# Causal mask inside VectorE's maximum pass, the first products of a batch in another order, and attend's hi and lo values made by GpSimd

## The reference

```python
x = _rmsnorm(hidden_states, ln1_w)
attn = _attention(x, Wq, Wk, Wv, Wo)
mod = MOD_SCALE * jnp.tanh(attn @ A)
h = _rmsnorm(residual, ln2_w)
gate_pre = h @ W_in_base.T + mod * (h @ A) @ B
gate = jax.nn.silu(gate_pre)
up = h @ W_up_base.T
mlp_out = gate * up @ W_down.T
return residual + mlp_out
```

```python
scores = jnp.einsum('bqhd,bkhd->bhqk', q, k) / np.sqrt(HD).astype(np.float32)
causal = jnp.tril(jnp.ones((s, s), bool))
scores = jnp.where(causal, scores, jnp.finfo(scores.dtype).min)
probs = jax.nn.softmax(scores, axis=-1)
```

## Time and profile before

| | us |
|---|---|
| median of 3 runs | 1052.58 (1052.24 to 1052.77) |
| the profiled execution's own time | 1054.3 |
| its span in the profile | 1052.6 |
| busy in it: PE | 1022.9 (97%) |
| PE weight loads | 851.5 (81%) |
| DVE | 702.6 (67%) |
| ACT | 601.6 (57%) |
| POOL | 269.6 (26%) |

### The profile page before, as it was taken

The page is one execution under the profiler, slowest core; times in us unless marked ns, Lnnn a source line. Parts: engine busy times, 40 slices in busy tenths (PEclk is TensorE's granted clock), DMA queues, the critical chain, the costliest instruction groups (busy, mean ns, idle before and its releaser), DMA issues.

```text
span 1052.6 us, 17255 instructions
## 1 busy us (share of the span) xinstructions
PE 1022.9 (97%) x5332; PEld 851.5 (81%) x5333; DVE 702.6 (67%) x1597; ACT 601.6 (57%) x1463; POOL 269.6 (26%) x252
## 2 busy tenths in 40 slices
PE   6899999999999999999999999999999999999998
PEld 6787888887888888878888888778888888788887
DVE  7766755996665558985665479966655589854443
ACT  4464555896444447985444368963344579753432
POOL 4536124662000116650000146510001166400000
PEclk9999999999999999999999999999999999999999
DMA  6534133343322425443322353532234254322221
GB/s 238 194 145 169 40 120 81 89 95 145 104 90 90 130 64 164 91 123 128 105 90 90 110 150 86 125 125 90 90 100 148 62 146 91 95 80 90 90 90 51
DMA packets 47079, 115.84 MB, mean 110 GB/s; under 512 B 6800, under 2 KB 6800, under 8 KB 46096
## 3 DMA queue, kind: packets, MB, share of 16 engines
q1 hardware_dynamic: 43968, 105.06, 33.4%
q0 software_dynamic: 3040, 9.96, 2.7%
HBM read 76.46 MB, written 13.37 MB: 85 GB/s over the span
## 4 chain that ended last, share of the span: by engine, by line
PE 86%; DVE 6%; DMA 2%; issue 2%; POOL 2%; ACT 1%; SPq 1%; DVEq 0%; POOLq 0%; ACTq 0%
PE bank L525 67%; PE bank L727 5%; PE bank L764 5%; PE bank L688 3%; DVE wr L1386 2%; DMA stack<-wr 2%; DVE nb L1398 1%; PE bank L816 1%; PE bank L692 1%; POOL big L497 1%; DMA big<-in_x,gidx 1%; PE bank L581 1%; SPq L320 1%; PE bank L596 1%; PE bank L639 1%
## 5 line engine op out<-in xcount | busy, mean ns | idle before, releaser
L525 PE MATMUL bank<-hT,wr 128*128 128x512 f32 x1488 | 358.2, 390 | 0.0
L525 PEld LDWEIGHTS bank<-hT,wr 128*128 128x128 f32 x1488 | 279.2, 188 | 60.6 <-issue 1.3
L525 PE MATMUL bank<-wr,actr 128*128 128x512 f32 (+1 forms) x1224 | 302.5, 397 | 2.5 <-DVE actr L1368 1.5
L525 PEld LDWEIGHTS bank<-wr,actr 128*128 128x128 f32 x1224 | 228.4, 190 | 51.0 <-issue 3.4
L497 POOL TENSOR_SCALAR big<-big,rr 128x256 f32<-128x256 f32 (+1 forms) x128 | 156.3, 1230 | 111.4 <-DVE rr L1403 111.0
L1434 DVE SCALAR_TENSOR_TENSOR wr<-stream,lns,wr 128x256 fp32r<-128x256 f32 x256 | 121.6, 537 | 51.1 <-ACT wr L1062 51.1
L436 POOL TENSOR_TENSOR wqs<-wstage,wqs 128x512 fp32r<-128x512 f32 x32 | 42.8, 1348 | 432.4 <-ACT wqs L938 431.0
L1386 DVE TENSOR_TENSOR wr<-bank,wr 128x512 fp32r<-128x512 f32 (+1 forms) x224 | 125.9, 607 | 28.8 <-ACT wr L938 28.1
L938 ACT ACTIVATE wr<-bank 128x512 fp32r<-128x512 f32 (+1 forms) x224 | 113.1, 536 | 53.3 <-PE bank L525 30.9
L1023 ACT ACTIVATE big<-bank,nb 128x512 f32<-128x512 f32 (+3 forms) x256 | 132.3, 546 | 5.5 <-DVE nb L1398 5.5
L938 ACT ACTIVATE actr<-act_sb 128x512 fp32r<-128x512 f32 x64 | 40.5, 633 | 145.7 <-DVE act_sb L1448 145.7
(11 more groups left out here) (179 smaller groups left out, 1025.2 us busy)
## 6 DMA issues: line engine op xcount, KB each, us to landing
stream<-in_wmlp SPq DMA_DIRECT2D x64, 512.0 KB, 4.0
stack<-wr SPq DMA_DIRECT2D x192, 128.0 KB, 2.3
stream<-in_wmlp SPq DMA_DIRECT2D x64, 256.0 KB, 2.7
big<-in_x SPq DMA_DIRECT2D x4, 1024.0 KB
big<-y_rows SPq DMA_DIRECT2D x4, 1024.0 KB, 5.6
residual<-big SPq DMA_DIRECT2D x4, 1024.0 KB
big<-residual SPq DMA_DIRECT2D x4, 1024.0 KB, 5.8
out<-big SPq DMA_DIRECT2D x3, 1024.0 KB, 4.8
```

The lines of the kernel that those rows point to most:

```text
L525: mm = pe.matmul(dst, lhs(pl, k), rhs(pr, k), start=start and i == 0, stop=stop and i == n - 1, skip_group_check=skip)
```

## The change

- The mask products go, and with them `identr`, `maskr` and `zeror`. GpSimd fills `masks` (128x512: zeros, and in its last 128 columns the triangle of -1e30).
- `maxima` is a `tensor_tensor_reduce` for each piece: scores from PSUM plus `masks`, times -1, written to `prob` in SBUF, and the minimum of that (the negated maximum) to `nb`, which now has two halves by the parity of the head. The built program has two instructions for each, the pass and one that writes the minimum. It also waits for `p_turned` of the head two before, whose probabilities lie in the same buffer.
- The exponentials read `prob` and write it in place, with scale -1. TensorE's next scores wait for `nb_ok`, no longer for `exp_ok`.
- Values: GpSimd makes hi and lo (`values_of`), after a multiply of its own, at the same heads as before. The copy of the second half of the values (`vpb_ok`) moves into VectorE's first head step, and uses bank 7.
- First products: the low-rank product leaves the start of the batch for heads 13 and 14 (four products each, bank 2), with its sums at the end of the stage. The second key projection goes into bank 5 (`SECOND_K`) and is split before the head steps, so `COPY_AT` loses its first entry; projections, values and scores at the start change order, and the scores of head 2 come ahead of the first turn.
- The up product of the first chunk has four parts of three products, in heads 9 to 12, and in each head step what fills (`filling`) stands behind the attends and the last scores.
- VectorE's four batches are written out.

The diff, cut to what the prediction speaks of:

```diff
-VALUES, LOW_RANK = (6, 4), 5
+VALUES, SECOND_K, LOW_RANK = (6, 7), 5, 2
...
-COPY_AT = {(0, 0): (1, 1), (0, 2): (2, 0), (1, 0): (2, 1), (1, 2): (3, 0), (2, 0): (3, 1)}
+COPY_AT = {(0, 2): (2, 0), (1, 0): (2, 1), (1, 2): (3, 0), (2, 0): (3, 1)}
...
-UP_PARTS = 6
-UP_FROM = H - 1 - UP_PARTS
+UP_PARTS, UP_FROM = 4, 9
+LOW_RANK_FROM = H - 3
...
+            def values_of(b, q):
+
+                if q < 2:
+                    pool.wait_ge(vpa_ok, b + 1)
+                    pool.wait_ge(vpb_ok, b + 1)
+                else:
+                    pool.wait_ge(pv_done, (b * NQ + q - 1) * QH)
+                rows, high = vp_v[:, :, 2 * q:2 * q + 2, :], vst_v[:, q % 2, :, :, HI, :]
+                g.tensor_copy(high, rows).then_inc(vst_hi, 1)
+                pool.wait_ge(vst_hi, b * NQ + q + 1)
+                g.tensor_tensor(vst_v[:, q % 2, :, :, LO, :], rows, high.bitcast(F32), ALU.subtract).then_inc(vst_lo, 1)
...
                         if q < NQ - 1 or j < QH - 1:
                             normalise((b * NQ + q) * QH + j + 1)
+                        if q == 0 and j == 0:
+                            values_of(b, 0)
+                        elif j == 2 and q < NQ - 1:
+                            values_of(b, q + 1)
...
-                    pe.wait_ge(exp_ok, n * 4 - 3)
+                    pe.wait_ge(nb_ok, n * 4 - 3)
                 score_rows(par, 3, True)
-                mask(0, 3 * P, 1)
...
+            def low_rank_part(b, half):
+
+                if half == 0:
+                    pe.wait_ge(nb_ok, (b + 1) * H * 4)
+                for k in (2 * half, 2 * half + 1):
+                    for part in (HI, LO):
+                        mm = pe.matmul(bank[LOW_RANK][:, :], apad[:, k, :], hT[:, part, k, :],
...
-                for qt, maxima in ((3, 1), (2, 3), (0, 3), (1, 4)):
-                    act.wait_ge(nb_ok, n * 4 + maxima)
...
-                    a.activation(prob[par][:, at:at + w], bank[bk][:, col:col + w], ACT.Exp,
-                                 bias=nb[:, qt:qt + 1], accum_out=rs[:, par, qt:qt + 1]).then_inc(exp_ok, 1)
+                for i, qt in enumerate((3, 2, 0, 1)):
+                    act.wait_ge(nb_ok, n * 4 + i + 1)
+                    rows = prob_rows(par, qt)
+                    a.activation(rows, rows, ACT.Exp, bias=nb[:, par, qt:qt + 1], scale=-1.0,
+                                 accum_out=rs[:, par, qt:qt + 1]).then_inc(exp_ok, 1)
...
+                if not first:
+                    dve.wait_ge(p_turned, (n - 1) * 3)
                 for i, qts in enumerate(((3,), (2, 0), (1,))):
                     dve.wait_ge(s_done, n * 3 + i + 1)
                     for qt in qts:
                         bk, col, _ = SCORE[qt]
-                        v.reduce_max(nb[:, qt:qt + 1], bank[bk][:, col:col + P * (qt + 1)], AXX,
-                                     negate=True).then_inc(nb_ok, 1)
+                        v.tensor_tensor_reduce(prob_rows(par, qt), bank[bk][:, col:col + P * (qt + 1)],
+                                               masks[:, S - P * (qt + 1):S], -1.0, 3.0e38, ALU.add, ALU.min,
+                                               nb[:, par, qt:qt + 1]).then_inc(nb_ok, 1)
```

More of the change, by code:

```diff
@@ L867, in batch @@
                 pe.wait_ge(fin_out, b + 1)
-                for k in range(DT):
-                    for part in (HI, LO):
-                        mm = pe.matmul(bank[LOW_RANK][:, :], apad[:, k, :], hT[:, part, k, :],
-                                       start=k == 0 and part == HI, stop=k == DT - 1 and part == LO)
-                mm.then_inc(ha_done, 1)
                 pe.wait_ge(qk_lo, b * (NQ * 2) + 1)
                 values((0, 1))
-                pe.wait_ge(qk_lo, b * (NQ * 2) + 2)
+                project(b, 1, 0)
                 scores(b * H, 0, stack_loads(b, 0), first=True)
-                project(b, 1, 0)
+                project(b, 1, 1, SECOND_K)
                 scores(b * H + 1, 1, stack_loads(b, 1))
                 values((2, 3))
-                project(b, 1, 1)
+                scores(b * H + 2, 0, stack_loads(b, 2))
                 wait_probs(b * H)
@@ L1420, in head_step @@
                 if two_more:
-                    maxima(n + 2)
+                    maxima(n + 2, j % 2)
+                if q == 0 and j == 0:
+                    dve.wait_ge(vp_done, b * 2 + 2)
+                    v.tensor_copy(vp[:, 2:4, :, :].rearrange("p t h r -> p (t h r)"),
+                                  bank[VALUES[1]][:, :]).then_inc(vpb_ok, 1)
                 for i, (bk, w, at) in enumerate(TURNED_BANKS):
@@ L1522, in batch @@
                 gate_up_low(b, 0, 0)
-                dve.wait_ge(ha_low, b + 1)
-                v.tensor_tensor(haT, bank[LOW_RANK][0:R, :], att_low, ALU.add).then_inc(ha_ok, 1)
-                maxima(b * H)
+                dve.wait_ge(res_out, (b + 1) * 16)
+                maxima(b * H, 0, first=True)
                 gate_up_low(b, 1, 1)
@@ L1528, in batch @@
                 qk_low(b, 1, 0)
-                maxima(b * H + 1)
-                dve.wait_ge(vp_done, b * 2 + 2)
-                v.tensor_copy(vp[:, 2:4, :, :].rearrange("p t h r -> p (t h r)"),
-                              bank[VALUES[1]][:, :]).then_inc(vpb_ok, 1)
+                maxima(b * H + 1, 1, first=True)
+                qk_low(b, 1, 1, SECOND_K)
                 for q in range(NQ):
@@ L1653, in _ @@
             v.memset(slot(CARRIER), 0.0).then_inc(fin_out, 1)
-            with dve.Fori(0, NB - 1) as b:
-                batch(b, True)
-            batch(NB - 1, False)
+            for b in range(NB):
+                batch(b, b < NB - 1)
 def kernel(x, itok_BxS_13_99985, ctx_2048, g_xattn, g_ffn, L0_ffn_ln1_w, L0_ffn_ln2_w, L0_ffn_Wq, L0_ffn_Wk,
```

117 lines of the change are left out of this document (47 added, 70 removed).

## The result

| | before | changed |
|---|---|---|
| median | 1052.67 us (1051.64 to 1053.64) | 1047.7 us (1045.09 to 1048.88) |
| ratio | | 0.9946, 95% interval 0.9937 to 0.9956 |
| span of the profiled execution | 1052.6 us | 1044.3 us |
| busy: PE, DVE, ACT, POOL | 1022.9, 702.6, 601.6, 269.6 us | 1011.3, 701.9, 608.0, 284.6 us |

The changed kernel is 0.5% faster, where 1060.3 us and "slower" were forecast. To see where, I cut each batch at VectorE's reciprocals, one per head: from a batch's first to its third is the **start**, from there to the tenth the seven **early** steps, to the sixteenth the six **late** steps, and to the first of the next batch the **rest** (tail, chunks, next projections).

What follows compares the result with a forecast made beforehand. VectorE was to take over from TensorE as the attention stage's limit. Its last step 1.4 us late plus 0.47 at the tail gave 1.9 us a batch, 7.7 in four: 1060.3 us, range 1044 to 1087.

Steps and rivals of the forecast that it cites:

- I take 0.09, the row of the same kind: VectorE's read-out after each pass delays the next instruction 0.09 us, as on ScalarE; four make 0.36.
- The lower end, 0: Lower end of the read-out's price on VectorE: it might vanish behind the end of the pass, costing 0.
- The loop: Passes wait for transposes, which wait for VectorE's low halves: 0.25 us paid in VectorE-limited steps, except four with a half.
- T: VectorE's time for a head's four passes with their read-outs, taken at 1.95 us, range 1.83 to 2.39.
- rival 3: The masked pass on VectorE runs at half rate, 18 us a batch, 1133 us; chance 0.05.
- VectorE is the limit from the first head to the last: Attention head steps: VectorE's 4.33 and 4.68 us both exceed TensorE's 4.24, so TensorE's saving is idle time.
- rival 1: Masks pay: read-out hides behind its pass, next six steps at TensorE's 4.24, 1041 us; chance 0.25 including up to no change.
- Late it buys nothing: Taking the masks off TensorE, 0.24 us a head step, gains nothing in late steps, where TensorE waits.
- step 2: VectorE's third head step of a batch, counted from 0, predicted to begin at 412.6 us after the start's chain.
- That does not make head 0 earlier: Batch start: moving the low-rank products leaves head 0's scores waiting for stack loads; passes start near 395.05 instead of 394.97.
- The tail: Batch end: four low-rank products (0.94) replace two up products (0.47) before the last head's products, 0.47 us more.
- 0.5 for GpSimd: Third step: GpSimd's values and weights hold VectorE's next multiply by 0.9 us, 0.5 net per batch.

Runs made afterwards that it cites:

- the copies: Changed kernel with one small 128 x 1 copy behind each of the four passes on VectorE: 1059.79 us, 1.0059.
- the early copy: Changed kernel with VectorE's copy of the second two value tiles ahead of the first head step: 1042.65 us, 0.9897.
- values back and early copy: Changed kernel with hi and lo values on ScalarE and VectorE again, value copy ahead of the first head step: 1051.44 us, 0.9978.
- the late release: Changed kernel with TensorE waiting for the exponentials, not the passes alone, before writing next scores into a bank: 1063.96 us, 1.0108.

## Why the prediction was wrong, step by step

**The step that failed** is "I take 0.09, the row of the same kind" for the read-out. ScalarE's read-out delays the next instruction by 0.09; on VectorE the next pass starts with the read-out, and four passes with their read-outs take 1.65 us where 1.95 was forecast. The lower end, 0, stood in the text and decided the sign: at four times 0.06 more per step (the copies) the time is 1059.8, without them 1047.7. The nearest row in name was on another engine; the lower-end row, small instructions on VectorE itself, was nearer: its 0.06 is what each small copy cost in the experiment.

**The loop was right.** With T = 1.65 instead of 1.95 the text's sums are 0.85 + 1.65 + 1.53 = 4.03 and 0.20 + 0.40 + 0.60 + 1.65 + 1.53 = 4.38; measured were 4.02 and 4.38. With T = 1.90 they are 4.28 and 4.63; measured 4.25 and 4.61. The wait was there at its predicted size (0.84 against 0.85), and taking it away brought 7.2 us. The pass ran at the rate of the maxima (688 ns for 512 columns, against 684 for the maximum in the kernel before), so rival 3 is out. The rule of the Trainium skill (Vector Engine (DVE) Microarchitecture Reference, section 7) speaks of two SBUF sources; with one of them in PSUM these rows, of an instruction that the trace calls CUSTOM_DVE_ANT_0, show no halving.

**"VectorE is the limit from the first head to the last"** fell with it: early steps are 4.24 with TensorE alone in the chain, rival 1's number. "Late it buys nothing" was wrong by itself: without masks most late steps went from 3.85 to 3.73, the six from 23.92 to 23.30.

**The start.** The text had step 2's reciprocal at 412.6 - 398.27 = 14.33 us after the first. With three passes of 0.30 less it is 13.43; batches 0 and 2 of the changed kernel have 13.2, batch 1 has 13.71 with the lower clock, batch 3 14.0 behind a late stack load. GpSimd's cast and subtraction were taken at 0.40 and 0.75 and took 0.40 and 0.73, and VectorE's multiply behind the next values was held by 0.9 us, as forecast (1.39 instead of 0.49); whether 0.5 of it reached the time, as the sum has it, is not shown. "That does not make head 0 earlier" was true, but it made it later: 0.40 us from the gate products to the next batch's first reciprocal (148.83 instead of 148.44). What the prediction left out is that TensorE's wait for the values could cost its clock as well.

**The tail** was priced at 0.47 and took 0.43 (by the chain of waits 7.45 instead of 7.02 us from the last reciprocal to the gate products). The extra ScalarE copy and VectorE sum lay under the gate and up products, as predicted.

**The sum again.** By rival 1's working with T = 1.65, per batch: step 2 at 411.7, six steps of 4.24, five of 4.03 and one of 4.38, 0.5 for GpSimd, gives 462.2, 2.9 early; less 0.47, four times: 9.6 us less, about 1043. The spans of the two profiles differ by 8.3. Between the two numbers lie the later first reciprocal (0.4, three times) and the batch at the lower clock (1.0), which no part of the prediction had, partly made up by a start of 13.2 instead of 13.43 in two batches. The medians differ by 5.0 only. Of the 3.3 us between profiles and medians, 1.6 are the changed kernel's other runs, longer at a lower clock (1047.7 against 1046.06); the other 1.6 are on the side of before, whose profiled execution took 1054.3 where the median is 1052.67, and why is not shown.

## What to carry to other kernels

Price an instruction that the trace lacks by rows of the same engine before rows of the same name, and when one such price, times many, decides the sign, let it widen the chances and not only the range. A change with several parts can hide its best one: here leaving the masks off TensorE was worth 11.8 us, and a buffer shared with the transposes and one copy behind four passes cost 7.2 and 5.0 us when each is taken away alone, 7.9 when both are. Where TensorE will wait for a chain of three engines at one place, ask what the granted clock does behind that wait, and move what ends the chain.

## What the runs showed of the hardware that was not expected

- VectorE's accumulator read-out has a record of 83 ns and starts together with the next pass; pass and read-out together take at most 0.015 more than the plain maximum (1.65 against 1.59 us for four), while a 128x1 copy in the same place, 0.15 us long in the record, delays the next pass by 0.06.
- TensorE's clock behind a wait at the first step: after 0.32 and 1.2 us of idle time it stayed at 1.0, after 3.97 us it fell to 0.50 in all four batches. Between them it went either way. With the early copy it stayed at 1.0 after 1.2 to 1.6 us in all batches. After 2.1 us it fell in one batch of four in the changed kernel and in two with both low-rank halves in head 13, after 2.35 us with the small copies in two, after 2.65 us (2.16 in batch 3) with values back and early copy in all four. And it fell in all four after 1.57 us with the late release, where TensorE had already waited twice (0.38 and 0.33 us) in the 6 us before. The idle stretch alone did not decide it.
